# One core's vision tower: 128-row solve of a delta-rule scan, 64-column products in place of narrow ones, and products of ones moved into waits

## The chip, the core and the metric

The kernel runs on one core of a Trainium2 chip. TensorE (PE) multiplies matrices, VectorE (DVE) and ScalarE (ACT) work on rows, GpSimd (POOL) adds, and SyncE (SP) issues the transfers. The metric is the device time of the core in microseconds. Everything is float32. An f32 product on PE is two LDWEIGHTS/MATMUL pairs, so the profile counts two MATMUL records for each call of `mm`.

## The reference, cut to what matters

64 images of 84 x 84 pixels become 4 patch tokens and one class token each, with C = 256 channels: a convolution, attention over nine positions of each window, and a class attention. Then two layers of an attention with a delta rule, each followed by a gated product with 704 inner channels, and at the end a feed-forward part whose operands are rounded to FP4 values. The delta rule runs over sequences of 64 steps and 8 heads of 32 channels:

```python
def step(S, inps):
    qi, ki, vi, bi = inps
    pred = jnp.einsum('bhkv,bhk->bhv', S, ki)
    S = S + bi[..., None, None] * ki[..., :, None] * (vi - pred)[..., None, :]
    o = jnp.einsum('bhkv,bhk->bhv', S, qi)
    return (S, o)
...
for l in range(L):
    h = rmsnorm(x, norm1_w[l])
    x = x + delta_attn(h, Wq[l], Wk[l], Wv[l], Wb[l], Wo[l], onorm_w[l])
    h = rmsnorm(x, norm2_w[l])
    gy = h @ Wg[l]
    g, y = jnp.split(gy, 2, axis=-1)
    x = x + jax.nn.silu(g) * y @ Wd[l]
```

## The kernel before

The order of every engine's work is written out by hand, and semaphores join the engines. PE has one list: the convolution (six groups, L1313), keys and values of the nine positions (L1357, L1371), statistics (`stat`, L1345), class attention (`both_windows`, L1416 and L1420), two times `layer(l)`, and the last stage (L1860 to L1926). PE is mostly fed in time by the others.

The scan over 64 steps is not run step by step. For each of 40 pairs of sequence group and head (NG = 20 column groups on two halves of the partitions) the kernel forms the 64 x 64 matrix of key products, `per_window` (L1707), and solves a triangular system. The 64 steps are two blocks of 32 rows. So the 128 partitions hold four quarters of 32 rows: quarters 0 and 2 are the early blocks, 1 and 3 the late ones. Each half of the 20 groups (b = 0, 1, NB = 10 groups) lies in a PSUM bank of its own.

- The inverse T of each 32 x 32 block is made by doubling in a loop, `pe.Fori(0, LEVELS - 1)`, four rounds: `level_y` (L1736) for both halves, ACT copies (L503), `level_z` (L1745) for both halves, and DVE's masked copy and transpose (L1158, L1161). Each half of each is 40 products of 32 x 32, on all four quarters, 80 records. In the code the loop stands once: 320 record pairs.
- After the loop PE makes the query norms' first halves, two products of 320 columns (L1760, banks 2 and 3).
- `solve((0, 2), b)` (L1767) multiplies T with the values on the early quarters, 20 products for each half. ACT copies quarter 0 (L545), DVE quarter 2 (L1178), 32 rows each.
- The couplings (L1782) give what the early block adds to the late one. DVE adds it in four operations of 32 rows (L1184).
- `solve((1, 3), b)` does the late quarters, with copies by ACT (L548) and DVE (L1188).
- `outputs(0)`, `outputs(1)` (L1801), 40 products. ACT squares them (L551), two products with `blk` complete the norms (L1813), ACT takes Ln and Exp (L329, L331), DVE scales (L1198), PE projects (L1819) and DVE adds the residual (L1203). Between L1198 and L1203 DVE rounds a piece of the FP4 weights (L670, L674, L675). `weights_across` (L1458) are transposes of those weights.

Ahead of the loop stand the projections, `betas` (L1676, L1680; 8 and 4 columns), `key_squares` (L1689, L1691; 4 columns), `per_window`, and the value products (L1720 and L1723, then L1727). `keep_clock` (L1471) and `keep_clock_briefly` (L1476) are products of ones that nobody reads.

## Time and profile before

| what | us |
|---|---|
| median of three runs | 298.47 |
| the three runs | 296.54, 298.47, 299.1 |
| profiled execution, device time | 295.59 |
| its span, first to last instruction | 293.8 |
| mean granted TensorE clock in it | 0.959 of 2.4 GHz |

Times in the rows below are microseconds from the start of the span. A row of the timeline merges neighbouring instructions of one line: start, busy time, engine, line, operation, tiles, rows*columns of the array, shapes, number of records; in brackets the engine's idle time before the first of them and what ended it. "issue" means that the profile shows nothing that the engine waited for.

### The profile page before, as it was taken

To read this page: it belongs to the slowest core of one execution; us is meant where nothing else is said; L and a number is where in the kernel's file an instruction comes from. 1 tells how busy PE (TensorE), PEld (TensorE's weight loads), DVE (VectorE), ACT (ScalarE), POOL (GpSimd) and SP (SyncE) were. 2 spreads that over 40 slices of the span, in tenths; PEclk is the share of its full clock that TensorE was granted. 3 is DMA by queue.
4 is the path that set the end of the run, shared out by engine and by line. 5 is a ranking of instruction groups with operands and counts; after the bars stand their busy time and mean duration, and the time that the engine had idled before them with its cause. 6 is when DMAs were issued, how large, how long until landed. Compare 5 with 4: busy or idle time off the path is not lost.

```text
span 293.8 us, 9910 instructions
## 1 busy us (share of the span) xinstructions
PE 268.0 (91%) x4473; PEld 205.8 (70%) x4473; DVE 201.4 (69%) x402; ACT 96.9 (33%) x243; POOL 38.0 (13%) x35
## 2 busy tenths in 40 slices
PE   8999999999999899968879999978889999788855
PEld 8566678778997788857756766858776676655543
DVE  3649869977689666467668588466676663688761
ACT  1122301330000126656134432755324423462310
POOL 1991100203992000000000000000000000000000
PEclk9999999999999999999959999897995999999988
DMA  7999900000000000000004006200000000000001
GB/s 287 417 424 418 444 20 0 0 0 2 0 0 2 1 2 1 2 4 0 4 2 140 7 1 220 85 2 2 1 7 0 0 2 0 1 0 2 0 10 34
DMA packets 2730, 18.71 MB, mean 64 GB/s; under 512 B 464, under 2 KB 784, under 8 KB 1936
## 3 DMA queue, kind: packets, MB, share of 16 engines
q1 hardware_dynamic: 2704, 18.34, 15.8%
q8 instruction: 20, 0.33, 0.4%
q14 instruction: 6, 0.05, 0.1%
HBM read 18.01 MB, written 0.33 MB: 62 GB/s over the span
## 4 chain that ended last, share of the span: by engine, by line
PE 77%; DVE 14%; ACT 4%; issue 2%; DMA 2%; SPq 0%; DVEq 0%
PE ps L1313 12%; PE ps L1635 8%; PE ps L1357 5%; PE ps L1847 4%; PE ps L1371 4%; PE ps L1889 3%; PE ps L1616 3%; PE ps L1736 3%; PE ps L1745 3%; DMA big<-in_patches 2%; DVE big L1161 2%; DVE wt L1158 2%; PE ps L1303 2%; PE ps L1813 2%; PE ps L1819 2%
## 5 line engine op out<-in xcount | busy, mean ns | idle before, releaser
L1313 PE MATMUL ps<-big,cwb 128*128 128x384 f32 x112 | 37.9, 489 | 0.0
L1313 PEld LDWEIGHTS ps<-big,cwb 128*128 128x128 f32 x112 | 20.9, 190 | 13.0 <-DVE cwb L766 0.3
L1635 PE MATMUL ps<-xT,wl 128*128 128x320 f32 x88 | 24.5, 434 | 1.1 <-ACT wguT L373 1.1
L293 POOL TENSOR_TENSOR xs<-xs,big 128x640 f32<-128x640 f32 x14 | 23.3, 1665 | 1.4
L1635 PEld LDWEIGHTS ps<-xT,wl 128*128 128x128 f32 x88 | 16.6, 190 | 8.2 <-ACT wguT L373 1.6
L1736 PE MATMUL ps<-wt,big 32*32 32x32 f32 x1280 | 14.7, 199 | 5.2 <-DVE wt L1115 2.4
L349 ACT COPY pecT<-ps 128x384 f32<-128x384 f32 x12 | 5.7, 479 | 40.7 <-PE ps L1313 40.7
L1736 PEld LDWEIGHTS ps<-wt,big 32*32 32x32 f32 x1280 | 13.1, 110 | 7.4 <-DVE big L1161 4.0
L1371 PE MATMUL ps<-wt,pecT 128*128 128x256 f32 x72 | 16.5, 381 | 0.6 <-DVE big L871 0.6
L1357 PE MATMUL ps<-wt,pecT 128*128 128x256 f32 x72 | 16.9, 381 | 0.0
L1158 DVE COPY_PREDICATED wt<-cst,ps 128x320 f32<-128x320 int32 x16 | 8.0, 500 | 11.5 <-PE ps L1745 11.5
L1371 PEld LDWEIGHTS ps<-wt,pecT 128*128 128x128 f32 x72 | 13.5, 190 | 2.9 <-DVE big L871 1.0
L1357 PEld LDWEIGHTS ps<-wt,pecT 128*128 128x128 f32 x72 | 13.5, 190 | 2.3
L1745 PE MATMUL ps<-wt,big 32*32 32x32 f32 x1280 | 13.4, 196 | 1.4 <-issue 1.4
L1745 PEld LDWEIGHTS ps<-wt,big 32*32 32x32 f32 x1280 | 12.5, 107 | 1.6 <-issue 1.6
L1847 PE MATMUL ps<-big,wl 128*128 128x320 f32 x48 | 13.4, 435 | 0.0
L776 DVE TENSOR_REDUCE part<-pecT 128x128 f32<-128x384 f32 x12 | 7.1, 594 | 8.7 <-ACT pecT L349 8.6
L1219 DVE TENSOR_TENSOR cwb<-ps,cwb 128x320 f32<-128x320 f32 (+1 forms) x12 | 5.9, 490 | 9.9 <-PE ps L1635 5.7
L1847 PEld LDWEIGHTS ps<-big,wl 128*128 128x128 f32 x48 | 8.8, 190 | 4.2 <-DVE big L1211 1.0
L503 ACT COPY wt<-ps 128x320 f32<-128x320 f32 x16 | 6.8, 425 | 14.6 <-PE ps L1736 14.6
L300 POOL TENSOR_TENSOR sq<-sq 128x384 f32<-128x384 f32 x6 | 6.3, 1051 | 39.9 <-ACT sq L342 39.9
L1889 PE MATMUL ps<-wguT,pecT 128*128 128x352 f32 x32 | 10.0, 466 | 1.1 <-ACT pecT L596 1.1
(310 smaller groups left out, 533.8 us busy)
## 6 DMA issues: line engine op xcount, KB each, us to landing
big<-in_patches SPq DMA_DIRECT2D x6, 960.0 KB, 11.8
wl<-in_layers SPq DMA_DIRECT2D x2, 2176.0 KB, 19.8
wf<-in_ffn SPq DMA_DIRECT2D x1, 2112.0 KB, 17.8
wl<-in_layers SPq DMA_DIRECT2D x2, 1040.0 KB, 15.9
wt<-in_tok SPq DMA_DIRECT2D x1, 1536.0 KB, 24.7
wt<-in_tok SPq DMA_DIRECT2D x1, 768.0 KB, 8.4
cwb<-in_conv SPq DMA_DIRECT2D x1, 640.0 KB, 3.9
cst<-in_constants SPq DMA_DIRECT2D x1, 320.0 KB, 25.0
```

Of the source, the lines that this page charges most:

```text
L293: nc.gpsimd.tensor_tensor(xs[:, hf], old, new, ALU.add).then_inc(S["xsum"], 1)
L776: step(v.tensor_reduce(part[:, min(g % 3, 1), c, :], pecT[:, c, g * GRP:(g + 1) * GRP].rearrange("p (t n) -> p n t", t=3), AX.X, ALU.add))
L1158: v.copy_predicated(tc_[:, g, :], m.unsqueeze(1).broadcast_to([P, NB, 32]), bank32(6 + b, slice(0, P))).then_inc(S["tp"], 1)
L1313: last = mm(ps[:, i % 4, 0:GRP], cwc[:, k, c * P:(c + 1) * P], xg[:, g, k, :], start=(k == 0), stop=(k == KC - 1))
L1357: last = mm(ps[:, 4 + un % 2, t * C:(t + 1) * C], pecT[:, c, i * P:(i + 1) * P], wkv[:, c, 0:C], start=(c == 0), stop=(c == CH - 1))
L1371: last = mm(ps[:, un % 3, t * C:(t + 1) * C], pecT[:, c, i * P:(i + 1) * P], wkv[:, c, C:2 * C], start=(c == 0), stop=(c == CH - 1))
L1616: last = mm(ps[:, bank, cols], lw(at)[:, c, j * P:(j + 1) * P], src[:, c, cols], start=(c == 0), stop=(c == CH - 1))
L1635: last = mm(ps[:, bank, 0:NT], w(c, j), x[:, c, :], start=(c == 0), stop=(c == CH - 1))
L1736: last = mm(ps[r, 4 + b, 32 * k:32 * k + 32], apm[r, NB * b + k, own], tc_[r, NB * b + k, :], start=True, stop=True)
L1745: last = mm(ps[r, 6 + b, 32 * k:32 * k + 32], ttc[r, NB * b + k, :], yc[r, NB * b + k, :], start=True, stop=True)
L1847: last = mm(ps[:, 6 + j, 0:NT], wd[:, i, j * P:(j + 1) * P], act[:, i, :], start=(i == 0), stop=(i == FC - 1))
L1889: last = mm(ps[:, b + w, 0:352], xqT[:, c, P * p:P * p + P], wguT[:, c, 352 * w:352 * w + 352], start=(c == 0), stop=(c == CH - 1))
```

## The change

1. The solve. `solve(b)` works on all four quarters, both times, so the first one also makes unused values on the late quarters and the second one repeats the early ones. One ACT copy of 128 rows takes half b = 0, one DVE copy of 128 rows half b = 1, both times. For the additions to cover 128 rows, the couplings get a second product for each old one, with a stationary operand of zeros (`nought`), which writes zeros under the early quarters; one DVE addition replaces two. The query norms' second product moves behind the second solve.
2. 64 columns (`WIDE`) replace 1, 4 or 8 moving columns where nobody reads the further ones: `stat`, the first products of `both_windows`, `betas` (the first four), `key_squares`, and the norms of the last stage (L1866). `ug` moves into a stretch of `wt` so that 64 columns can be read.
3. Products of ones: 512 instead of 192 columns in the front ahead of `group_scores(1)`; 512 columns between the value products of each layer; 256 columns behind the outputs of each layer; in the last stage two of seven go between the weight transposes, and 256 columns come behind the first output product.
4. ACT makes the causal masks 8 to 11 before its first copy of the loop instead of after.

```diff
+WIDE = 64
+        nought = sb("nought", [P, 32])
-        ug = sb("ug", [P, CH, H])
+        ug = wt[:, T_GQ:T_GQ + 512].rearrange("p (c n) -> p c n", c=CH)
-        def half(x, q, b):
-
-            return x[32 * q:32 * q + 32, NB * b:NB * (b + 1), :].rearrange("p g n -> p (g n)")
+        def part_of(x, b):
+
+            return x[:, NB * b:NB * (b + 1), :].rearrange("p g n -> p (g n)")
-        heads = blk.rearrange("p (h d) -> p h d", h=HP)[:, :, 0]
+        heads = blk.rearrange("p (h d) -> p h d", h=HP)[:, :, 0:WIDE // HP]
...
+            nc.gpsimd.memset(nought[:, :], 0.0)
...
+                causal(8, 12)
                 y_out(1, 0)
...
-                causal(8, 12)
                 y_out(1, 1)
...
-                for b in range(2):
-                    act_.wait_ge(S["u1_mm"], EACH["u1_mm"] * l + b + 1)
-                    nc.scalar.copy(half(uc, 0, b), ps[0:32, 4 + b, 0:NT]).then_inc(S["u1"], 1)
-                for b in range(2):
-                    act_.wait_ge(S["u2_mm"], EACH["u2_mm"] * l + b + 1)
-                    nc.scalar.copy(half(uc, 1, b), ps[32:64, 4 + b, 0:NT]).then_inc(S["u2"], 1)
+                act_.wait_ge(S["u1_mm"], EACH["u1_mm"] * l + 1)
+                nc.scalar.copy(part_of(uc, 0), ps[:, 4, 0:NT]).then_inc(S["half_0"], 1)
+                act_.wait_ge(S["u2_mm"], EACH["u2_mm"] * l + 1)
+                nc.scalar.copy(part_of(uc, 0), ps[:, 4, 0:NT]).then_inc(S["half_0"], 1)
...
-                v.tensor_scalar(nsse, ps[:, 0, 0:NG], EPS_RMS, -1.0, ALU.add, ALU.mult).then_inc(S["ss"], 1)
+                sums = ps[:, 0, 0:PJ * WIDE].rearrange("p (g d) -> p g d", g=NG)[:, :, 0]
+                v.tensor_scalar(nsse, sums, EPS_RMS, -1.0, ALU.add, ALU.mult).then_inc(S["ss"], 1)
...
-                for b in range(2):
-                    dve.wait_ge(S["u1_mm"], EACH["u1_mm"] * l + b + 1)
-                    v.tensor_copy(half(uc, 2, b), ps[64:96, 4 + b, 0:NT]).then_inc(S["u1_two"], 1)
-
+                dve.wait_ge(S["u1_mm"], EACH["u1_mm"] * l + 2)
+                v.tensor_copy(part_of(uc, 1), ps[:, 5, 0:NT]).then_inc(S["half_1"], 1)
                 for b in range(2):
                     dve.wait_ge(S["r_mm"], EACH["r_mm"] * l + b + 1)
-                    for a in range(2):
-                        q = 2 * a + 1
-                        v.tensor_tensor(half(bv, q, b), half(bv, q, b), ps[32 * q:32 * q + 32, 6 + b, 0:NT], ALU.add
-                                        ).then_inc(S["b2"], 1)
-                for b in range(2):
-                    dve.wait_ge(S["u2_mm"], EACH["u2_mm"] * l + b + 1)
-                    v.tensor_copy(half(uc, 3, b), ps[96:128, 4 + b, 0:NT]).then_inc(S["u2_two"], 1)
+                    v.tensor_tensor(part_of(bv, b), part_of(bv, b), ps[:, 6 + b, 0:NT], ALU.add
+                                    ).then_inc(S["half_1"], 1)
+                dve.wait_ge(S["u2_mm"], EACH["u2_mm"] * l + 2)
+                v.tensor_copy(part_of(uc, 1), ps[:, 5, 0:NT]).then_inc(S["half_1"], 1)
...
-                    last = mm(ps[:, 7, at:at + 1], sq[:, 0, t * P:(t + 1) * P], ones[:, 0:1], start=True, stop=True)
+                    last = mm(ps[:, 7, at:at + WIDE], sq[:, 0, t * P:(t + 1) * P], ones[:, 0:WIDE], start=True, stop=True)
...
-                    mm(ps[:, b, at:at + n], stat[:, c, P * hf:P * hf + P], moving(c), start=(c == 0), stop=(c == CH - 1))
+                    mm(ps[:, b, at:at + WIDE], stat[:, c, P * hf:P * hf + P], moving(c, WIDE), start=(c == 0),
+                       stop=(c == CH - 1))
...
-            keep_clock(0, 1, 192)
+            keep_clock(0, 1, 512)
...
-                            last = mm(ps[:, 5, H * p:H * p + H], hT[:, c, P * p:P * p + P], wb[:, c, :],
+                            at = L_B + H * c
+                            last = mm(ps[:, 5, H * p:H * p + WIDE], hT[:, c, P * p:P * p + P], wl[:, at:at + WIDE],
...
-                        mm(ps[:, 0, HP * pj:HP * pj + HP], kqsq[:, 0, pj % 2, P * p:P * p + P], heads, start=True, stop=True)
+                        mm(ps[:, 0, WIDE * pj:WIDE * (pj + 1)], kqsq[:, 0, pj % 2, P * p:P * p + P], heads, start=True,
+                           stop=True)
...
                 last.then_inc(S["v_mm"], 1)
+                keep_clock(5, 1, 512)
                 for c in range(CH):
                     last = mm(ps[:, 7, 0:C], hT[:, c, 0:P], wvb[:, c, :, 0:P], start=(c == 0), stop=(c == CH - 1))
...
-                for j in range(CH):
+
+                def query_norms(j):
+
                     mm(ps[:, 2 + j, 0:NT], blk, kqsq[:, 1, j, :], start=True, stop=False)
 
-                def solve(rows, b):
+                query_norms(0)
+
+                def solve(b):
 
                     for g in range(NB * b, NB * (b + 1)):
-                        for q in rows:
+                        for q in range(4):
...
-                    solve((0, 2), b).then_inc(S["u1_mm"], 1)
+                    solve(b).then_inc(S["u1_mm"], 1)
                 pe.sem_inc(S["t"], -2)
                 for b in range(2):
-                    pe.wait_ge(S["u1"], EACH["u1"] * l + b + 1)
-                    pe.wait_ge(S["u1_two"], EACH["u1_two"] * l + b + 1)
+                    if b:
+                        pe.wait_ge(S["half_1"], EACH["half_1"] * l + 1)
+                    else:
+                        pe.wait_ge(S["half_0"], EACH["half_0"] * l + 1)
                     for g in range(NB * b, NB * (b + 1)):
+                        cols = slice(32 * (g % NB), 32 * (g % NB) + 32)
                         for a in range(2):
-                            last = mm(ps[64 * a + 32:64 * a + 64, 6 + b, 32 * (g % NB):32 * (g % NB) + 32],
-                                      apm[64 * a:64 * a + 32, g, 32:64], uc[64 * a:64 * a + 32, g, :],
-                                      start=True, stop=True)
+                            early, late = slice(64 * a, 64 * a + 32), slice(64 * a + 32, 64 * a + 64)
+                            mm(ps[early, 6 + b, cols], nought[late, :], uc[late, g, :], start=True, stop=True)
+                            last = mm(ps[late, 6 + b, cols], apm[early, g, 32:64], uc[early, g, :], start=True, stop=True)
                     last.then_inc(S["r_mm"], 1)
                 for b in range(2):
-                    pe.wait_ge(S["b2"], EACH["b2"] * l + 2 * b + 2)
-                    solve((1, 3), b).then_inc(S["u2_mm"], 1)
+                    pe.wait_ge(S["half_1"], EACH["half_1"] * l + b + 2)
+                    solve(b).then_inc(S["u2_mm"], 1)
+                query_norms(1)
+
...
                 outputs(1).then_inc(S["o_mm"], 2)
+                keep_clock(5, 1, 256)
...
-            weights_across(6, 9)
-            keep_clock(5, 7)
+            weights_across(6, 8)
+            keep_clock(5, 2)
+            weights_across(8, 9)
+            keep_clock(5, 5)
...
                 last.then_inc(S["out_mm"], 1)
+                if p == 0:
+                    keep_clock(4, 1, 256)
```

## Rows read from the trace of the kernel before

**Rows 1.** The page: busy time of the engines (part 1), DMA queues (3), the chain (4).
```profile
PE 268.0 (91%) x4473; PEld 205.8 (70%) x4473; DVE 201.4 (69%) x402; ACT 96.9 (33%) x243; POOL 38.0 (13%) x35
...
q8 instruction: 20, 0.33, 0.4%
...
PE 77%; DVE 14%; ACT 4%; issue 2%; DMA 2%; SPq 0%; DVEq 0%
```

**Rows 2.** PE's timeline from the loop's end; the last line is layer 1.
```profile
140.07 1.57 PE L1745 MATMUL ps<-wt,big 32*32 32x32 f32 x160
141.88 1.31 PE L1760 MATMUL ps<-pecT,cst 128*128 128x320 f32 x4 [0.24 <-issue]
143.13 1.45 PE L1767 MATMUL ps<-wt,big 32*32 32x32 f32 x80
...
149.32 1.70 PE L1801 MATMUL ps<-big,wt 64*32 64x64 f32 x80 [0.69 <-DVE wt L1188]
151.61 2.50 PE L1813 MATMUL ps<-wt,cst 128*128 128x320 f32 x4 [0.59 <-ACT wt L551]
...
219.09 1.60 PE L1801 MATMUL ps<-big,wt 64*32 64x64 f32 x80 [0.69 <-DVE wt L1188]
```

**Rows 3.** DVE's timeline in the same stretch of layer 0.
```profile
145.49 2.04 DVE L1184 TENSOR_TENSOR wt<-wt,ps 32x320 f32<-32x320 f32 x4 [0.37 <-PE ps L1782]
...
155.12 0.55 DVE L1198 SCALAR_TENSOR_TENSOR big<-ps,vec,wt 128x320 f32<-128x320 f32 x1 [0.45 <-ACT wt L331]
```

**Rows 4.** PE's timeline where it stops on "issue"; the last four are layer 1.
```profile
127.67 0.89 PE L1736 MATMUL ps<-wt,big 32*32 32x32 f32 x80 [1.40 <-DVE wt L1115]
...
129.26 1.20 PE L1745 MATMUL ps<-wt,big 32*32 32x32 f32 x115 [0.28 <-issue]
...
197.09 0.50 PE L1745 MATMUL ps<-wt,big 32*32 32x32 f32 x36
198.70 1.65 PE L1745 MATMUL ps<-wt,big 32*32 32x32 f32 x124 [1.11 <-issue]
...
214.62 0.88 PE L1782 MATMUL ps<-wt,big 32*32 32x32 f32 x44
215.66 0.76 PE L1782 MATMUL ps<-wt,big 32*32 32x32 f32 x36 [0.15 <-issue]
```

**Rows 5.** Windows: stretch, length, busy time of engines, granted clock, DMA share, GB/s.
```profile
126.90:127.10 0.20, 0.00 (x0) 0.00 (x0) 0.17 (x1) 0.20 (x2) 0.00 (x0) 1.00 0.31 82
130.30:130.50 0.20, 0.17 (x18) 0.05 (x6) 0.17 (x2) 0.03 (x1) 0.00 (x0) 1.00 0.35 82
131.00:142.00 11.00, 9.64 (x961) 9.00 (x962) 7.83 (x17) 5.91 (x19) 0.00 (x0) 1.00 0.00 0
143.10:143.30 0.20, 0.20 (x11) 0.17 (x12) 0.00 (x0) 0.00 (x0) 0.00 (x0) 1.00 0.27 82
...
195.80:196.00 0.20, 0.00 (x0) 0.00 (x0) 0.20 (x1) 0.20 (x2) 0.00 (x0) 1.00 0.45 82
...
213.10:213.30 0.20, 0.20 (x12) 0.18 (x13) 0.00 (x0) 0.00 (x0) 0.00 (x0) 1.00 0.32 82
```

**Rows 6.** The page's granted clock in 40 slices (7.3 us each), and two windows.
```profile
PEclk9999999999999999999959999897995999999988
...
148.00:154.70 6.70, 5.36 (x114) 3.88 (x109) 4.27 (x7) 2.61 (x7) 0.00 (x0) 0.50 0.01 2
...
189.00:192.30 3.30, 3.30 (x83) 2.64 (x72) 1.51 (x4) 2.50 (x9) 0.00 (x0) 0.50 0.02 5
```

**Rows 7.** PE's timeline: one-column and 64-column products, and L1707 in both layers.
```profile
45.31 2.07 PE L1345 MATMUL ps<-ones,sq 128*128 128x1 f32 x18
...
111.32 1.10 PE L1605 MATMUL ps<-gag,wt 128*128 128x64 f32 x8
...
121.05 1.56 PE L1707 MATMUL ps<-pecT 32*64 32x128 f32 x80
...
188.78 2.44 PE L1707 MATMUL ps<-pecT 32*64 32x128 f32 x80
```

More of the change, by code:

```diff
@@ L930, in class_keys @@
                 dve.wait_ge(S["u"], 1)
-                v.tensor_tensor(ug[:, :, :], u[:, :, :],
+                v.tensor_tensor(ug[:, :, 0:H], u[:, :, :],
                                 vec[:, V_GKG:V_GKG + 2].unsqueeze(2).broadcast_to([P, CH, H]), ALU.mult
@@ L1419, in both_windows @@
                     for c in range(CH):
-                        last = mm(ps[64 * a:64 * a + 64, b, at + n:at + 2 * n], stat[:, c, cols], moving(c),
+                        last = mm(ps[64 * a:64 * a + 64, b, at + n:at + 2 * n], stat[:, c, cols], moving(c, n),
                                   start=(c == 0), stop=(c == CH - 1))
@@ L1428, in group_scores @@
                 pe.wait_ge(S["k_free"], 10)
-                both_windows(5, 2 * H * hf, H, lc[:, 1], lambda c: ug[:, c, :], hf).then_inc(S["gsc_mm"], 1)
+                both_windows(5, 2 * H * hf, H, lc[:, 1], lambda c, n: ug[:, c, 0:n], hf).then_inc(S["gsc_mm"], 1)
             def group_stats(hf):
@@ L1436, in group_stats @@
                     pe.wait_ge(S["rk"], 4)
-                both_windows(7, 100 + 2 * hf, 1, sql, lambda c: ones[:, 0:1], hf).then_inc(S["gst_mm"], 1)
+                both_windows(7, 100 + 2 * hf, 1, sql, lambda c, n: ones[:, 0:n], hf).then_inc(S["gst_mm"], 1)
             def group_values(hf):
@@ L1688, in key_squares @@
                         p = pj // 2
-                        mm(ps[:, 0, HP * pj:HP * pj + HP], kqsq[:, 0, pj % 2, P * p:P * p + P], heads, start=True, stop=True)
+                        mm(ps[:, 0, WIDE * pj:WIDE * (pj + 1)], kqsq[:, 0, pj % 2, P * p:P * p + P], heads, start=True,
+                           stop=True)
                     for a in range(2):
-                        last = mm(ps[64 * a:64 * a + 64, 0, 4 * HP:5 * HP], kqsq[:, 0, a, NW:NT], heads, start=True, stop=True)
+                        last = mm(ps[64 * a:64 * a + 64, 0, 4 * WIDE:5 * WIDE], kqsq[:, 0, a, NW:NT], heads, start=True,
+                                  stop=True)
                     last.then_inc(S["ss_mm"], 1)
@@ L1803, in outputs @@
                     return last
-                for b in range(2):
-                    pe.wait_ge(S["u2"], EACH["u2"] * l + b + 1)
-                pe.wait_ge(S["u2_two"], EACH["u2_two"] * l + 2)
+                pe.wait_ge(S["half_0"], EACH["half_0"] * (l + 1))
+                pe.wait_ge(S["half_1"], EACH["half_1"] * (l + 1))
                 outputs(0).then_inc(S["o_first"], 1)
@@ L1865, in _ @@
                     n = P if p < 2 else 64
-                    last = mm(ps[0:n, p, 0:1], sqx[:, c, P * p:P * p + n], ones[:, 0:1], start=(c == 0), stop=(c == CH - 1))
+                    last = mm(ps[0:n, p, 0:WIDE], sqx[:, c, P * p:P * p + n], ones[:, 0:WIDE], start=(c == 0),
+                              stop=(c == CH - 1))
                     if c and p:
```

2 lines of the change are left out of this document (1 added, 1 removed).

## The prediction

> **What bounds the kernel now.** I read the page's totals first, then the chain of waits, then PE's timeline between the end of the doubling loop and the next projection. PE is busy for 91% of the span [rows 1] and the chain that ended last is PE's for 77% of it [rows 1], so the time is that of PE's list. The solve is a thinner place. In layer 0 the loop ends at 140.07 + 1.57 = 141.64, two wide products follow, then the 32x32 products of the first solve (80 records in L1767), the couplings L1782 (80), the second solve (80), and the outputs L1801, which start at 149.32 [rows 2]: 7.7 us for 244 records, most of it waiting for 32-row copies and additions such as the four of L1184, 2.04 us together [rows 3]. (An f32 product is two records.) The second thing to see is the granted clock: 0.50 (the 1.2 GHz level) from 148.0 to 154.7 and from 189.0 to 192.3, and by the slices of the page also near 199 to 203, near 220 to 226 and near the end [rows 6]. So it falls after both solves and after the tiny products of layer 1. The third thing is where the forecast is decided: PE's instructions arrive as a stream. The page counts 20 pieces of kind "instruction" with 0.33 MB, 16.4 KB each [rows 1]. Of 4,473 records 3 x 320 x 2 are repeats of a loop, so 2,553 stand in the code, 128 to a piece.
>
> Three times PE stopped in dense code with nothing to wait for ("issue"): inside L1745 in layer 0 for 0.28 us, at its record 36 in layer 1 for 1.11 us, and at record 44 of L1782 in layer 1 for 0.15 us [rows 4]. From the second stop to the third lie, in code, some 43 + 80 records of L1745, 4 of L1760, 80 of L1767 and 44 of L1782: 251, two pieces of 126 (a piece holds waits too). Each stop ends a fixed time after a piece began to land: pieces begin near 127.0, 195.9 and 213.2 [rows 5], PE goes on at 129.26, 198.70 and 215.66 [rows 4], so 2.3, 2.8 and 2.5 us later. After the first stop the next piece begins near 130.4 [rows 5], 1.1 us after PE went on. So I read: on entering piece k PE asks for piece k+1 alone, it begins to land 1.1 us later and can be used 3.35, 3.9 and 3.55 us after the request. No piece arrives while the loop repeats (0 GB/s from 131 to 142) [rows 5].
>
> **The change part by part.**
> (a) Solves on all four quarters. Records per layer: first solve 80 to 160, couplings 80 to 160 (the products of zeros), second solve 80 to 160, outputs 80. With four quarters 160 records took 1.57 us [rows 2], 9.8 ns each; with two, 80 took 1.45 us, 18 ns. So in array time twice the products cost nothing: 6 blocks of 0.78 us, 4.7 us. One 128-row copy replaces two 32-row ones, and one addition two, since 32 rows take as long (2.04 / 4 = 0.51 us in L1184) as 128 (0.55 in L1198) [rows 3]. One product of query norms, some 0.6 us [rows 2], moves behind the second solve, beside DVE's last copy. If code is free, outputs start 0.9 + 4.7 = 5.6 us plus 0.4 after 141.64, at 147.65 instead of 149.32: 1.7 us won per layer.
>
> But the same stretch is then 2 + 160 + 160 + 160 + 2 + 80 records straight through, 564 instead of 324. In layer 0 a piece began near 143.2 [rows 5], so PE entered piece A near 142.1, some ten records behind the loop; the next borders come 126, 252, 378 and 504 records later, the last at about record 30 of the outputs. A piece's content needs 126 x 9.8 ns = 1.2 us and the next one 3.4 us, so PE stops in every piece. B opens at 142.1 + 3.4 = 145.5 (in the first solve), C at 148.9 (couplings), D at 152.3 (second solve), E at 155.5 to 155.7. The last 50 records of the outputs, at the 21 to 24 ns that they show at the lower clock (80 in 1.70) [rows 2], end near 156.6. Before, they ended at 151.02; the following L1813 had its start at 151.61 and comes to 157.4: +5.8 us. Layer 1: A at 213.2 - 1.1 = 212.1, E at 212.1 + 4 x 3.5 = 226.1, outputs end at 227.2 instead of 219.09 + 1.60 = 220.69 [rows 2]: +6.5, and 0.2 for (c). Together +12.5 us. This puts code in the place of the copies' waits, which all fit into the stops. Behind the outputs nothing is denser than before. ACT's Ln and Exp, DVE's L1198, its three steps of weight rounding and the two additions of L1203 keep their distances.
>
> (b) Clock around the solves. In full-speed code (a) would also hold the clock at 2.4 GHz, worth about 1.2 us per layer: L1813 takes 2.50 us for what takes 1.31 in L1760 at the upper level [rows 2], and DVE's weight rounding between L1198 and L1203 takes part of that back. With stops in each piece PE has 1.2 us of work in 3.4 us, and the clock fell before in a stretch that held more, so I count nothing won.
>
> (c) Wide products of ones. 256 columns behind the outputs last 0.43 us at full clock, covered by the wait for ACT's square (0.59 us ahead of L1813) [rows 2]; at half clock 0.85, so 0.2 to 0.3 sticks out, counted above. 512 columns between the value products: 0.85 us under PE's wait for DVE, 1.40 us in layer 0 [rows 4]. But L1736's first half starts 0.8 us later, and in it PE enters the piece whose successor it then lacks in L1745; the request and the end of that stop move by about 0.75 us in layer 0. The front's 512 instead of 192: +0.05. In the last stage seven stay seven, and the new 256 lies in a wait for DVE: 0. Its fall at the end stays.
>
> (d) Columns 1, 4 or 8 made 64. Eighteen one-column records take 2.07 us, eight 64-column ones 1.10 us; less the 0.2 us that the end of the last one adds, 104 and 113 ns each [rows 7]. 104 records are widened (36 of L1345, 16 of the two windows, 16 betas, 24 squares of keys, 12 at the end): 1.0 us at most, nothing if the weight load sets the pace; I take 0.6, on the side of the row. In return the fall at 189.0 [rows 6], behind these products, should go: 80 records of L1707 would take 1.56 instead of 2.44 us [rows 7], -0.9, of which (c) gives back 0.4 as the code request is later; and the fall near 199 goes with the filled wait, -0.5 (an estimate: L1745 and L1736 are held back there less by the clock than by DVE).
>
> (e) Moving ug into wt, the order of ACT's causal masks, strided reads: covered by PE, 0.
>
> Sum on the profiled execution: 295.59 + 12.5 + 0.75 + 0.05 + 0.6 - 0.5 - 0.5 = 308.5 us. The runs' median, 298.47, is 2.9 above that execution. I carry 1 us of this over, since clock falls placed by chance will also be in the new one, and say 309.5. With 3.3 to 3.9 us per piece over eight pieces the sum moves by -1 to +3.5; with (d) at its ends by 0.6; so 305 to 315 for this case alone.
>
> A rule that speaks against my reading: the Trainium skill, "Runtime: NRT & Kernel Launch", section "Instruction fetch mechanics", says that code comes in 16 KiB blocks of 256 instructions, the next one fetched while the current one runs, and that this is mostly hidden because issue is slower than the refill. The size agrees (16.4 KB, 128 pairs). "Hidden" does not, at 9.8 ns a record: the three stops say so. By that rule the time would be that of the first rival.
>
> **The rivals.**
> 1. Code is on time (the stops of rows 4 have another cause, or several pieces can be asked for). For it: 160 records ran at 9.8 ns, and the chain gives "issue" 2% [rows 1]. Against it: those 160 were mostly a repeated loop, and the stops stand 251 records apart. Then: 2 x 1.7 won in the solves, 2 x 1.2 by the clock (DVE's rounding included), 1.4 by the falls at 189 and 199, 0.7 paid: 295.6 - 6.5 = 289, and with the offset 290 to 291. It is decided by whether a stretch of over 126 records in straight code at under 27 ns runs through. Faster.
> 2. Code delays only part: requests go out earlier since the queue runs ahead during waits, a piece takes 2 to 2.7 us instead of 3.4. Then E opens 8 to 10.8 us after 142.1 and the outputs end at 151 to 154, 0 to 2.7 us later than before in each layer: 297 to 302.
> 3. Widened columns cost 30 ns instead of 6, with the first rival's solve: 292 to 294.
> 4. The change doesn't do what it says (128-row operations cost more than 32-row ones): excluded by [rows 3].
>
> **How the numbers follow.** Forecast 0.72; rival 2 0.08 (half of it slower by over 1%, half within); rivals 1 and 3 together 0.20, of which 0.01 ends within 1%. Measurement can tell about 1% from no change. Slower 0.76, same 0.06, faster 0.18. The range reaches from 298 to 316: it holds the forecast's 305 to 315 and most of rival 2, and leaves out the first rival and tails, 0.2.
>
> **What would show it.** Right: in the solve PE has five pieces landing about 3.5 us apart, idle time of about 2 us called "issue" in the first solve, the couplings, the second solve and the outputs, and from the loop's end to L1813's counterpart 16 us instead of 10. Wrong: solve blocks back to back in under 6 us, pieces landing 1.5 us apart, and clock 1.0 behind the solves. The fall at 189 gone shows (d); the first stop of L1745 about 0.7 us longer in layer 0 shows (c).

## The result, and the profile after

| | before | after |
|---|---|---|
| median of the paired runs, us | 298.79 (4 runs) | 311.7 (4 runs) |
| lowest and highest, us | 296.54, 300.32 | 309.67, 312.33 |
| profiled execution, its span | 295.59, 293.8 | 309.67, 307.9 |
| mean granted TensorE clock in it | 0.959 | 0.945 |

The ratio is 1.0385, with a 95% interval from 1.0277 to 1.0493: the medians differ by 12.9 us, the profiled executions by 14.1 us. A fifth run of the changed kernel, outside the paired ones, took 307.38 us. Some runs of either kernel fall into a slower state, and the ratios, here and below, are those of the others.

The page of the changed kernel, the lines that answer to [rows 1] (busy time, the queue of code, the chain), and two of its groups of instructions: L1747 is the doubling loop's second part, L1773 the solve. After the bar stand busy time, mean ns of one, and the idle time before them with what ended it.

```profile
PE 275.1 (89%) x4963; PEld 209.0 (68%) x4963; DVE 197.5 (64%) x394; ACT 95.3 (31%) x239; POOL 38.0 (12%) x36
...
q8 instruction: 24, 0.39, 0.5%
...
PE 75%; DVE 14%; issue 6%; ACT 4%; POOL 0%; DVEq 0%; POOLq 0%
...
L1747 PE MATMUL ps<-wt,big 32*32 32x32 f32 x1280 | 13.5, 197 | 2.7 <-issue 2.7
L1773 PE MATMUL ps<-wt,big 32*32 32x32 f32 x640 | 8.9, 215 | 6.4 <-issue 6.4
```

PE has 490 more records and is busy 7.1 us longer, but the span grew by 14.1. "issue" on the chain went from 2% to 6%, and the solve alone lost 6.4 us to it. PE's timeline from the loop's end in layer 0, the answer to [rows 2]; the couplings L1792/L1793 alternate, and one of their rows stands for all, the one where PE went on after its stop:

```profile
143.03 0.78 PE L1764 MATMUL ps<-pecT,cst 128*128 128x320 f32 x2 [0.24 <-issue]
143.73 1.36 PE L1773 MATMUL ps<-wt,big 32*32 32x32 f32 x134
146.70 0.41 PE L1773 MATMUL ps<-wt,big 32*32 32x32 f32 x26 [1.60 <-issue]
...
150.30 0.26 PE L1793 MATMUL ps<-wt,big 32*32 32x32 f32 x1 [2.20 <-issue]
...
153.76 1.48 PE L1773 MATMUL ps<-wt,big 32*32 32x32 f32 x90 [1.57 <-issue]
155.17 1.44 PE L1764 MATMUL ps<-pecT,cst 128*128 128x320 f32 x2
156.53 1.95 PE L1812 MATMUL ps<-big,wt 64*32 64x64 f32 x80
158.41 1.22 PE L1469 MATMUL ps<-cst,ones 128*128 128x256 f32 x2
159.43 2.34 PE L1824 MATMUL ps<-wt,cst 128*128 128x320 f32 x4
```

Three stops of 1.60, 2.20 and 1.57 us, with nothing that PE waited for. Layer 1 has the same three (at 223.02, 226.89 and 230.35, of 1.60, 2.09 and 1.58 us). Windows of the same trace, each where a piece of PE's code begins to land in layer 0 (stretch, length, busy time of PE, its weight loads, DVE, ACT, POOL, granted clock, DMA share, GB/s):

```profile
144.20:144.40 0.20, 0.20 (x45) 0.20 (x36) 0.00 (x0) 0.00 (x0) 0.00 (x0) 1.00 0.29 82
147.90:148.10 0.20, 0.20 (x22) 0.08 (x10) 0.20 (x1) 0.00 (x0) 0.00 (x0) 1.00 0.30 82
151.30:151.50 0.20, 0.20 (x33) 0.20 (x25) 0.10 (x1) 0.00 (x0) 0.00 (x0) 0.50 0.35 82
154.80:155.00 0.20, 0.20 (x29) 0.20 (x19) 0.00 (x0) 0.00 (x0) 0.00 (x0) 0.50 0.33 82
158.20:158.40 0.20, 0.20 (x24) 0.04 (x6) 0.17 (x2) 0.00 (x0) 0.00 (x0) 0.50 0.29 82
```

Narrower windows put their beginnings at 144.33, 147.97, 151.43, 154.89 and 158.28, 3.4 to 3.6 us apart. PE goes on at 146.70, 150.30 and 153.76, which is 2.3 to 2.4 us after a piece began to land; before, 2.3 to 2.8 us were read from [rows 4, 5]. From one stop to the next PE runs 128 records (136 from the loop's end to the first stop, then 128 and 128). In the kernel before, the pieces behind the loop of layer 0 began at 143.2, 146.85 and 150.6, also about 3.7 us apart, but there PE ran out of them only once, for 0.15 us in layer 1 [rows 4].

Where the 14.1 us lie, by the start of the same work in the two traces (for the loop, the end of its last product), each time after less before:

| milestone | before | after | gap | grown by |
|---|---|---|---|---|
| first half of the loop's first product, layer 0 | 125.4 | 126.4 | 1.0 | 1.0 |
| loop's end, layer 0 | 141.6 | 142.8 | 1.2 | 0.2 |
| norms (L1813; L1824) | 151.6 | 159.4 | 7.8 | 6.6 |
| `per_window`, layer 1 | 188.8 | 196.6 | 7.8 | 0.0 |
| first half of the loop's first product, layer 1 | 194.4 | 201.7 | 7.3 | -0.5 |
| loop's end, layer 1 | 211.6 | 219.1 | 7.5 | 0.2 |
| norms, layer 1 | 221.3 | 235.3 | 14.0 | 6.5 |
| down projection, layer 1 | 241.9 | 254.5 | 12.6 | -1.4 |
| last output product's end | 291.0 | 305.1 | 14.1 | 1.5 |

So 13.1 of 14.1 us arise between the loops' ends and the norms.

### The profile page after: what moved, and what is told of

It is laid out like the page before. It is cut to its first block, busy times and chain, and to the rows that moved or that the text cites. A ratio compares the mean times of both kernels' runs of the same rounds, so it can differ in the third digit from the quotient of the medians.

```text
span 307.9 us, 10875 instructions
## 1 busy us (share of the span) xinstructions
PE 275.1 (89%) x4963; PEld 209.0 (68%) x4963; DVE 197.5 (64%) x394; ACT 95.3 (31%) x239; POOL 38.0 (12%) x36
## 4 chain that ended last, share of the span: by engine, by line
PE 75%; DVE 14%; issue 6%; ACT 4%; POOL 0%; DVEq 0%; POOLq 0%
PE ps L1310 12%; PE ps L1633 8%; PE ps L1354 5%; PE ps L1858 4%; PE ps L1368 3%; PE ps L1903 3%; PE ps L1614 3%; PE ps L1738 3%; PE ps L1773 3%; PE ps L1747 3%; PE ps L1474 2%; DVE big L1163 2%; PE ps L1937 2%; PE ps L1469 2%; DVE wt L1160 2%
## 5 line engine op out<-in xcount | busy, mean ns | idle before, releaser
L1633 PEld LDWEIGHTS ps<-xT,wl 128*128 128x128 f32 x88 | 16.6, 190 | 9.1 <-ACT wguT L376 2.4
L1738 PE MATMUL ps<-wt,big 32*32 32x32 f32 x1280 | 14.6, 198 | 4.1 <-DVE big L1163 2.4
L1738 PEld LDWEIGHTS ps<-wt,big 32*32 32x32 f32 x1280 | 12.9, 109 | 6.3 <-DVE big L1163 4.0
L1160 DVE COPY_PREDICATED wt<-cst,ps 128x320 f32<-128x320 int32 x16 | 8.0, 500 | 12.9 <-PE ps L1747 12.8
L1747 PE MATMUL ps<-wt,big 32*32 32x32 f32 x1280 | 13.5, 197 | 2.7 <-issue 2.7
L1773 PE MATMUL ps<-wt,big 32*32 32x32 f32 x640 | 8.9, 215 | 6.4 <-issue 6.4
L1747 PEld LDWEIGHTS ps<-wt,big 32*32 32x32 f32 x1280 | 12.6, 108 | 2.9 <-issue 2.9
L1469 PE MATMUL ps<-cst,ones 128*128 128x320 f32 (+2 forms) x36 | 13.7, 491 | 0.0
L1858 PE MATMUL ps<-big,wl 128*128 128x320 f32 x48 | 13.4, 435 | 0.0
L1773 PEld LDWEIGHTS ps<-wt,big 32*32 32x32 f32 x640 | 7.9, 125 | 7.7 <-issue 7.7
L506 ACT COPY wt<-ps 128x320 f32<-128x320 f32 x16 | 6.8, 426 | 16.4 <-PE ps L1738 16.4
## 6 DMA issues: line engine op xcount, KB each, us to landing
wf<-in_ffn SPq DMA_DIRECT2D x1, 2112.0 KB, 17.9
```

The lines of the kernel that those rows point to most:

```text
L1160: v.copy_predicated(tc_[:, g, :], m.unsqueeze(1).broadcast_to([P, NB, 32]), bank32(6 + b, slice(0, P))).then_inc(S["tp"], 1)
L1469: mm(ps[:, bank, 0:width], ones[:, :], cst[:, 0:width], start=True, stop=True)
L1633: last = mm(ps[:, bank, 0:NT], w(c, j), x[:, c, :], start=(c == 0), stop=(c == CH - 1))
L1738: last = mm(ps[r, 4 + b, 32 * k:32 * k + 32], apm[r, NB * b + k, own], tc_[r, NB * b + k, :], start=True, stop=True)
L1747: last = mm(ps[r, 6 + b, 32 * k:32 * k + 32], ttc[r, NB * b + k, :], yc[r, NB * b + k, :], start=True, stop=True)
L1773: last = mm(ps[r, 4 + b, 32 * (g % NB):32 * (g % NB) + 32], ttc[r, g, :], bv[r, g, :], start=True, stop=True)
```

## The experiments

The theory: PE's code comes in pieces of 16.4 KB (128 records with their weight loads, a few less where waits and a loop's end stand between them), one ahead at most, 3.4 to 3.9 us apart when PE would use them up faster, and the change grows the straight code behind each loop from 324 to 564 records. Rivals: the doubled products or the longer copies cost by themselves; the granted clock makes the loss; the wide products of ones do.

**1. The solve alone** (edit 1, without the wide products and the 64 columns).

```diff
-                    solve((0, 2), b).then_inc(S["u1_mm"], 1)
+                    solve(b).then_inc(S["u1_mm"], 1)
...
+                            mm(ps[early, 6 + b, cols], nought[late, :], uc[late, g, :], start=True, stop=True)
...
-                    solve((1, 3), b).then_inc(S["u2_mm"], 1)
+                    solve(b).then_inc(S["u2_mm"], 1)
```

> Only the solve is changed (four quarters, products of zeros, 128-row copies and additions, query norms split); columns, products of ones and the mask order are those of before. If code arrival is the cause (564 instead of 324 records behind each loop, some 27 ns a record), the kernel is as slow as the whole change: about 12 to 13 us over before, 310 to 312, with four stops on issue behind each loop. If the rest of the change (64 columns, products of ones) is the cause, it is at before's time less 3 us, 295 to 299.

Measured: 308.21 us (4 runs) against 297.84 (13 runs), ratio 1.0328 with an interval from 1.0257 to 1.0399. The solve carries most of the loss, but 2 us less of it than expected. The profiled execution took 312.53 us, more than the other three, so I take only places from it: stops in the first solve, the couplings and the second solve, and in layer 0 a short one (0.46 us) in the outputs.

**2. Everything but the solve** (edits 2 to 4; before's solve put back).

```diff
-                    solve(b).then_inc(S["u1_mm"], 1)
+                    solve((0, 2), b).then_inc(S["u1_mm"], 1)
...
+                    nc.scalar.copy(half(uc, 0, b), ps[0:32, 4 + b, 0:NT]).then_inc(S["u1"], 1)
```

> Everything but the solve is changed. Code arrival: within 1% of before, 298 to 300: the first stop in L1745 0.8 us longer in each layer, the low clock behind the narrow products of layer 1 gone, 0.6 us for wider columns. If the rest is the cause of the loss: 308 to 312.

Measured: 302.76 us (4 runs), ratio 1.0141 (1.0074 to 1.0209): 4 to 5 us, where the forecast's sum had 0.4. The expectation, 298 to 300 us, was missed. From the loops' ends to the norms it takes 10.6 and 10.8 us, before 10.0 and 9.7; the new product of 256 columns stands in this stretch, at the lower clock 1.22 us long in a wait of 0.59 us. PE's timeline of this kernel at the first stop in layer 0 and at layer 1's loop (L1743 and L1752 are the loop's two products):

```profile
129.45 0.56 PE L1752 MATMUL ps<-wt,big 32*32 32x32 f32 x43
131.37 1.22 PE L1752 MATMUL ps<-wt,big 32*32 32x32 f32 x117 [1.36 <-issue]
133.06 2.35 PE L1743 MATMUL ps<-wt,big 32*32 32x32 f32 x160 [0.47 <-DVE big L1163]
...
199.58 0.45 PE L1752 MATMUL ps<-wt,big 32*32 32x32 f32 x30
200.98 1.79 PE L1752 MATMUL ps<-wt,big 32*32 32x32 f32 x128 [0.95 <-issue]
204.43 0.26 PE L1752 MATMUL ps<-wt,big 32*32 32x32 f32 x2 [1.67 <-issue]
```

In layer 0 the stop is 1.36 us instead of 0.28 [rows 4]. In layer 1 a second border falls into the loop's first pass, two records before its end, and costs 1.67 us that neither before nor after paid. Three products of ones, six records, stand more in the code ahead of this place; before, the stop came after record 36 (now 30), and the rest of the pass, 124 records, ran through [rows 4].

**3. Between the two: the whole change with 404 records behind each loop** (the first solve stays on four quarters, no products of zeros, the second solve on two quarters).

```diff
-                            mm(ps[early, 6 + b, cols], nought[late, :], uc[late, g, :], start=True, stop=True)
...
-                    solve(b).then_inc(S["u2_mm"], 1)
+                    solve(b, (1, 3)).then_inc(S["u2_mm"], 1)
```

> The changed kernel without the products of zeros and with the second solve on the late quarters alone (the values added to the early quarters are then read by nobody): 404 records behind each loop instead of 564, all 128-row copies and additions kept. Code arrival: 160 x 27 ns = 4.3 us less in each layer, 302 to 304. If the products' own time on the array counts (9.8 ns a record, or the waits of copies): 160 x 9.8 ns = 1.6 us less in each layer, 308 to 309.

Measured: 305.68 us (4 runs), ratio 1.0269 (1.0208 to 1.033). The time lies between the two expectations. From loop's end to norms: 13.4 us in both layers. With the whole change (16.6 and 16.2) and experiment 2 (10.6 and 10.8), 564, 404 and 324 records take 16.4, 13.4 and 10.7 us in the mean: 240 records cost 5.7 us, 24 ns each, but unevenly, the first 80 of them 34 ns each and the other 160 19 ns, where 27 ns were expected for each. A piece of 128 records each 3.5 us would be 27 ns. Products that are left out take no array time either, so this alone doesn't separate code from products; experiments 5 and 6 do.

**4. The whole change with 324 records behind each loop** (both solves on two quarters, the 128-row copies and additions kept).

```diff
-                    solve(b).then_inc(S["u1_mm"], 1)
+                    solve(b, (0, 2)).then_inc(S["u1_mm"], 1)
...
-                            mm(ps[early, 6 + b, cols], nought[late, :], uc[late, g, :], start=True, stop=True)
...
-                    solve(b).then_inc(S["u2_mm"], 1)
+                    solve(b, (1, 3)).then_inc(S["u2_mm"], 1)
```

The further rows that the copies take here carry values that nobody reads.

> As the one before, and the first solve on the early quarters alone: 324 records as before the change, with 128-row copies and additions (they also carry values that nobody reads). Code arrival: some 7 us less in each layer than the changed kernel, and against the kernel with the rest alone only 0.5 to 1 us a layer, since the code of 324 records (8.7 us) sets the pace: 297 to 298.5. If copies set the pace: 1.7 us less in each layer than the rest alone, 295 to 296.

Measured: 298.46 us (11 runs), ratio 1.0013 (0.9972 to 1.0055). Taking the 240 records away gives back the whole 13 us, with every copy at 128 rows. Long copies are not the loss. This kernel differs from that of experiment 2 (1.0141) only in the solve's copies, additions and the place of one query-norm product; experiment 9 finds 0.2% for the copies and additions alone. So the prices of the parts don't simply add, and why this one is 1.3% faster was not taken apart.

**5 and 6. The same 256 tiny products, straight and in a loop**, put into the kernel before ahead of the layers, where nothing waits for them. Their values are read by nobody.

```diff
+            tiny_products(256)
```

```diff
+            with pe.Fori(0, 4):
+                tiny_products(64)
```

> The kernel before with 256 more 32x32 products of ones (512 records, unread) ahead of layer 0, written out. Price of code by itself. If a piece of 126 records is asked for only when the one ahead of it is entered, their last ones run at 3.4 to 3.9 us per 126 records: the stretch takes 12 to 14 us, broken by three or four stops on issue of about 2 us, with pieces landing about 3.4 us apart. If code is on time: 512 x 9.8 ns = 5.0 us without a stop.

> The same 512 records as a loop of four rounds over 64 products (128 records in the code). If code arrival sets the pace: one stop at most in the first round, then rounds of 1.25 us plus the branches, 6 to 9 us in all, so 5 to 7 us less than written out. If the products' own time sets the pace: both take the same.

Measured, one execution each: 314.1 and 304.88 us. PE's timeline of the straight ones:

```profile
115.33 2.09 PE L1855 MATMUL ps<-ones 32*32 32x32 f32 x225
119.73 1.27 PE L1855 MATMUL ps<-ones 32*32 32x32 f32 x128 [2.31 <-issue]
123.45 1.93 PE L1855 MATMUL ps<-ones 32*32 32x32 f32 x128 [2.46 <-issue]
127.18 0.65 PE L1855 MATMUL ps<-ones 32*32 32x32 f32 x31 [1.80 <-issue]
```

and of the looped ones:

```profile
117.22 1.29 PE L1855 MATMUL ps<-ones 32*32 32x32 f32 x128
118.66 4.10 PE L1855 MATMUL ps<-ones 32*32 32x32 f32 x384 [0.16 <-issue]
```

The 512 records take 12.5 us in straight code and 5.5 us in the loop. The straight ones come in bursts of exactly 128 behind a first one of 225 (the rest of one piece and the whole next one), with 3.7 us from the start of one to the next (119.73, 123.45, 127.18). Engine, waits, operands and products are the same in the two. One thing follows from the stops: the granted clock is 1.00 throughout the loop and 0.50 from 122 on in the straight code, where a burst takes 1.93 instead of 1.27 us. That is 0.7 us in this burst, and the three stops are 6.6 us together. What costs is that the code is new. The whole kernels differ by 9.2 us; the 2.2 us outside this stretch were not followed up.

**7. The borders moved.** 45 products of ones instead of 35 at the start of the kernel, in a wait: 20 records more ahead of everything, so every border comes 20 records earlier.

```diff
-            keep_clock_briefly(7, 35)
+            for _ in range(45):
+                mm(ps[0:32, 7, 0:50], ones[:, 0:32], ones[:, 0:50], start=True, stop=True)
```

> The changed kernel with ten more small products (20 records) at the very start, where PE waits for the first patches (45 of 50 columns in place of 35 of 64): everything behind lies 20 records later against the borders of the code pieces. Code arrival: the first stop in the loop's second product group moves from record 43 to 47 to about record 23 to 27, a new stop of about 2 us appears near record 310 of the loop's first round, and behind the loop the stop at record 134 of the first solve is gone, the others come 20 records earlier; 1.6 us are lost in each loop and 1.7 won behind it, so the time stays within 1% of the changed kernel, 309 to 312. If the stops have to do with what is computed there, they stay at the same products.

Measured: 311.07 us (4 runs), ratio 1.0488 (1.0437 to 1.0538). PE's timeline (L1748 is the loop's second product, L1774 the first solve):

```profile
128.77 0.38 PE L1748 MATMUL ps<-wt,big 32*32 32x32 f32 x23
130.10 1.30 PE L1748 MATMUL ps<-wt,big 32*32 32x32 f32 x128 [0.95 <-issue]
134.10 0.28 PE L1748 MATMUL ps<-wt,big 32*32 32x32 f32 x9 [2.70 <-issue]
...
147.20 1.58 PE L1774 MATMUL ps<-wt,big 32*32 32x32 f32 x160
```

The stop after record 43 of the loop's product moved to record 23, 20 earlier. A new stop of 2.70 us appeared 128 records on, inside the loop's first pass, and the stop in the first solve is gone in layer 0: its 160 records run through. In layer 1 it moved from record 139 to 119. The stops follow the borders, not the work. The expected balance did not come out: the loops' first passes lost more, and the ratio is 1.0% above that of the whole change.

**8. The clock held up in the stops.** After the first half of the first solve and behind each half of the couplings a product of ones, 512 columns wide.

```diff
+                    if b == 0:
+                        keep_clock(0, 1, 512)
...
+                    keep_clock(0, 1, 512)
```

> The changed kernel with one product of ones of 512 columns behind the first half of the first solve and behind each half of the couplings, placed into the stops: tells the clock from the code. If code sets the pace, the pieces stay 3.4 to 3.6 us apart and only what runs at the lower clock behind the solve (second query norm, outputs, norms, transposes) gets shorter: 1 to 2 us less in each layer, 308 to 310. If the low clock is what makes the solve slow: 6 us less in each layer, 300.

Measured: 308.9 us (4 runs), ratio 1.0396 (1.033 to 1.0461). The page's clock slices of this kernel:

```profile
PEclk9999999999999999999989999999997999999979
```

The mean clock rose to 0.982, above the 0.959 of the kernel before, and the ratio is that of the whole change. From the loops' ends to the norms it took 17.1 and 16.4 us, although the clock was low for 3.4 us there in layer 0 and hardly at all in layer 1 (with the change as it is, about 11 and 10 us). In layer 1 the pieces still began 3.3 to 3.8 us apart. In layer 0 they were 3.3 to 4.2 us apart, since the three products take time of their own. The low clock accompanies the loss and doesn't make it. What the clock gives is read behind the norms of layer 0: from there to the down projection it took 19.1 us, with the change as it is 19.9.

**9. The 128-row copies and additions alone**, in the kernel before, with its 324 records behind each loop and no further products.

```diff
-                for b in range(2):
-                    dve.wait_ge(S["u1_mm"], EACH["u1_mm"] * l + b + 1)
-                    v.tensor_copy(half(uc, 2, b), ps[64:96, 4 + b, 0:NT]).then_inc(S["u1_two"], 1)
+                dve.wait_ge(S["u1_mm"], EACH["u1_mm"] * l + 2)
+                v.tensor_copy(part_of(uc, 1), ps[:, 5, 0:NT]).then_inc(S["half_1"], 1)
...
-                        v.tensor_tensor(half(bv, q, b), half(bv, q, b), ps[32 * q:32 * q + 32, 6 + b, 0:NT], ALU.add
+                    v.tensor_tensor(part_of(bv, b), part_of(bv, b), ps[:, 6 + b, 0:NT], ALU.add
```

The late quarters' rows in the first copies, and the early ones' in the additions, carry values that nobody reads.

> The kernel before with one change: 128-row copies and additions in the solve, the products and their count as before (324 records behind each loop); the further rows carry values that nobody reads. If copies set the pace of the solve, 1.7 us less in each layer: 294 to 295. If code arrival takes over once the copies are short (324 records need about 8.7 us, the stretch takes 10.0 now): 0.5 to 1 us less in each layer, 296 to 297.

Measured: 296.53 us (12 runs) against 297.33 (17 runs), ratio 0.9983 (0.9948 to 1.0018). PE's timeline (L1765 solve, L1784 couplings, L1802 outputs):

```profile
144.10 1.45 PE L1765 MATMUL ps<-wt,big 32*32 32x32 f32 x80
145.44 1.14 PE L1784 MATMUL ps<-wt,big 32*32 32x32 f32 x54
147.09 0.59 PE L1784 MATMUL ps<-wt,big 32*32 32x32 f32 x21 [0.51 <-issue]
...
147.63 2.16 PE L1765 MATMUL ps<-wt,big 32*32 32x32 f32 x74
150.48 1.70 PE L1802 MATMUL ps<-big,wt 64*32 64x64 f32 x80 [0.69 <-DVE wt L1181]
```

(Some records are missing from this trace.) PE waits for no copy or addition until the outputs, but it stops for 0.51 us on its code, and the second solve's 74 records take 2.16 us at the lower clock, which came at 147.4. The outputs start 7.9 us behind the loop's end (142.61), against 7.7 before [rows 2]; in layer 1 it is 7.2 against 7.5.

**10. Experiment 2 without the 512 columns between the value products.**

```diff
-                keep_clock(5, 1, 512)
```

> The kernel with everything but the solve changed (measured at 1.014 of before), without the 512 columns of ones between the value products. If these cost by the later code request (first stop in L1745 longer by 0.8 to 1.3 us) and by the lower clock that follows it in the loop: 3 us less, 299 to 300, and no clock fall inside the loop of layer 0. If the 64-column products are what costs: no change, 302 to 303.

Measured: 296.5 us (10 runs) against 296.69 (23 runs), ratio 0.9977 (0.9945 to 1.001). That is 3 us below what was expected. The one product of 512 columns in each layer carries the whole 1.4% of experiment 2. PE's timeline of this kernel in the two layers:

```profile
129.01 0.58 PE L1751 MATMUL ps<-wt,big 32*32 32x32 f32 x45
130.19 1.58 PE L1751 MATMUL ps<-wt,big 32*32 32x32 f32 x115 [0.61 <-issue]
...
197.38 0.47 PE L1751 MATMUL ps<-wt,big 32*32 32x32 f32 x34
198.54 1.77 PE L1751 MATMUL ps<-wt,big 32*32 32x32 f32 x126 [0.70 <-issue]
```

The stops are 0.61 and 0.70 us, against 1.36 and 0.95 + 1.67 in experiment 2. In layer 1 the border that experiment 2 met two records before the end of the pass now lies just behind it. The second half of the expectation was wrong: the clock does fall inside the loop of layer 0, from 130.6 to 134.0, for as long as in experiment 2 (133.0 to 136.4). In layer 1 it is low for 3.4 us instead of 6.8. The stops explain 2.7 of the 6.0 us between the two traces, and another 1.7 us lie in the last stage, where the clock was low from 266.2 to 269.5 in experiment 2 and not here; what made that fall isn't shown. The 64-column products are all still in: with the fall at 189 that went with them, they cost nothing that can be measured.

**11. The clock kept without delaying the loop**: the kernel before with edit 2's 64 columns (all but `stat`), edit 4, and three products of ones of 256 columns in waits of the solve (behind the couplings, behind the second solve, behind the outputs).

```diff
+                keep_clock(0, 1, 256)
                 for b in range(2):
                     pe.wait_ge(S["b2"], EACH["b2"] * l + 2 * b + 2)
                     solve((1, 3), b).then_inc(S["u2_mm"], 1)
+                keep_clock(0, 1, 256)
...
+                keep_clock(5, 1, 256)
```

> The kernel before with products of ones of 256 columns in three waits of the solve (behind the couplings, the second solve and the outputs; 6 records a layer), and 64 columns in betas, key squares and the class windows, nothing else. If the clock can be kept up behind the solve at so little code: the falls at 148 and 220 are gone or shorter, L1813 takes 1.1 to 1.3 us instead of 2.5, the fall at 189 is gone, 2 to 4 us less: 294 to 296. If code arrival takes it back (stop in the couplings longer): 297 to 298.

Measured: 296.24 us (12 runs) against 296.69 (23 runs), ratio 0.9983 (0.9953 to 1.0013), just above the first expectation. The norms ran at the upper level:

```profile
153.14 0.70 PE L1474 MATMUL ps<-cst,ones 128*128 128x256 f32 x2
153.83 1.34 PE L1823 MATMUL ps<-wt,cst 128*128 128x320 f32 x4
```

1.34 us for what took 2.50 [rows 2], and from the loop's end to the down projection 28.6 us in both layers against 30.0 and 30.2 before. But the clock was low from 129.6 to 136.4 and from 197.9 to 208 instead, inside the loops. In this trace the gain went there: from the loop's first product to its end it took 17.9 and 19.5 us in the two layers, before 16.2 and 17.2.

**12. Experiments 9 and 11 together**: the short chain of copies with the clock kept, one product of ones behind the second solve and one behind the outputs.

```diff
-                keep_clock(0, 1, 256)
                 for b in range(2):
-                    pe.wait_ge(S["b2"], EACH["b2"] * l + 2 * b + 2)
-                    solve((1, 3), b).then_inc(S["u2_mm"], 1)
+                    pe.wait_ge(S["half_1"], EACH["half_1"] * l + b + 2)
+                    solve(b, (1, 3)).then_inc(S["u2_mm"], 1)
                 keep_clock(0, 1, 256)
```

> The two harmless halves together: before's sparse solve (324 records behind each loop) with 128-row copies and additions as in the run of the copies alone (1.00 of before), and the clock held through the solve by products of ones 256 columns wide in its waits as in the run with the clock kept (1.00 of before). Each alone gave nothing back at the end of the kernel. If what the copies save (two copies and two additions per layer fewer in a row, 0.5 to 1 us per layer) had only been lost to the low clock that followed, it shows now: 294.5 to 295.5 us against 296.7, ratio 0.993 to 0.996. If the code stop in the second part of the solve and the falls of the clock inside the loop take it back as they did in the two runs: 296 to 297.5, ratio 0.997 to 1.003.

Measured: 294.31 us (6 runs) against 297.31 (11 runs), ratio 0.9899 (0.9839 to 0.9958). It beats the kernel before by 1.0%, a little more than expected, and stands 4.9% of before's time below the changed one. PE's timeline of layer 1:

```profile
213.02 1.45 PE L1771 MATMUL ps<-wt,big 32*32 32x32 f32 x80
214.36 1.52 PE L1790 MATMUL ps<-wt,big 32*32 32x32 f32 x80
215.77 1.52 PE L1771 MATMUL ps<-wt,big 32*32 32x32 f32 x80
217.23 0.70 PE L1467 MATMUL ps<-cst,ones 128*128 128x256 f32 x2
217.98 1.44 PE L1809 MATMUL ps<-big,wt 64*32 64x64 f32 x80
219.35 0.70 PE L1467 MATMUL ps<-cst,ones 128*128 128x256 f32 x2
220.03 1.34 PE L1821 MATMUL ps<-wt,cst 128*128 128x320 f32 x4
```

This is what edit 1 was after, with half of the changed solve's products: solve, couplings and second solve back to back, norms 8.6 us behind the loop's end (9.7 before) and at the upper level. In layer 0 the clock still fell at 129.3 and at 149.8, and the norms came 9.7 us behind the loop. That the fall in layer 1's loop stayed away here and not in experiment 11 wasn't taken apart.

## Why the prediction was right, and where its terms were off

**Sign and mechanism: right.** The forecast was pieces about 3.5 us apart, PE stopped in the solve, the couplings and the second solve, and 16 us instead of 10 from the loop's end to the norms. Measured were 16.6 and 16.2 us, with pieces at 144.33, 147.97, 151.43, 154.89 and 158.28, 3.4 to 3.6 us apart. Of the four stops forecast behind each loop three came; the one in the outputs stayed away (see (a)). The runs leave no rival beside it: the same products cost 5.5 us looped and 12.5 straight (experiments 5 and 6), the stops move with the borders (7), without the 240 records the loss is gone (4), and with the clock at 0.982 it stays (8).

**The size of a piece** was taken at 126 records. That came from a stretch that holds a loop's end and waits; behind the loop it was 128, and the borders still fell within a few records of their forecast places.

**Rival 1 (code is on time) fell** by the stops at the borders. Its test, "a stretch of over 126 records runs through", was set too low, since the rest of one piece and the whole next one can be there already: 134 records ran through in the first solve, 160 in that of experiment 7 and 225 in experiment 5, and behind each PE stopped. The Trainium skill, "Runtime: NRT & Kernel Launch", section "Instruction fetch mechanics", calls the crossing of a 16 KiB boundary mostly hidden. In this kernel it is hidden in the first 118 us, the convolution and what follows, where PE shows no wait on "issue"; it costs 1.6 to 2.2 us in the changed solve, where 128 records take 1.3 us.

**Rival 2 (a piece in 2 to 2.7 us) fell**: no two pieces were closer than 3.3 us. **Rival 3 (64 columns cost 30 ns each) fell**: experiment 10 holds all of them and is at 0.9977, and in the last stage six records of one column took 0.81 us and six of 64 columns 0.92 (L1866, now L1877), 18 ns more each. **Rival 4**: a 128-row copy on DVE took 0.49 us (L1179, L1185) and on ACT 0.43 (L549), as the 32-row ones.

**Terms of the sum.**

- (a) Forecast +5.8 and +6.5 us, measured +6.6 and +6.5. In layer 0 two things were sized wrongly. The moved query-norm product was to lie beside DVE's last copy at 0.6 us; it took 1.44 us at the lower clock and ended behind that copy (155.28 + 0.49 = 155.77, the product 156.61). And the outputs, forecast to stop once more for piece E, show no stop in the changed kernel: their border fell near 157.2 (the next piece begins to land at 158.28, 1.1 us later), 2.3 us after E began to land at 154.89, when E had just become usable.
- (b) Nothing won by the clock around the solves: right in layer 0 (low from 148.3 to 162.0). In layer 1 it came back at 233.6, before the norms, and gave 1.4 us, which the last stage lost again (low for 6.8 us near the end, before for 3.4).
- (c) The first stop was forecast 0.75 us longer in layer 0: it went from 0.28 to 1.12 us, +0.84. In layer 1 it went from 1.11 to 1.56, +0.45 (forecast 0.4). But in experiments 2 and 10, with before's solve, the same 512 columns made the difference between 1.0141 and 0.9977. The sum had no term for a border that falls into the loop's first pass, or for the clock that falls with a longer stop. Within the whole change part of this is covered: experiments 1 and 2 add to 4.7%, the whole change is 3.85%.
- (d) Taken at 0.6 us; up to `per_window` of layer 0 the trace has 0.3 us (121.35 against 121.05), the front's wider product included. That the fall at 189 [rows 6] goes was right: `per_window` in layer 1 took 1.63 us instead of 2.44 [rows 7]. That the fall near 199 goes, forecast at -0.5 us, was wrong: it came later instead, behind the longer first stop, and just as long. The window in the changed kernel, with the granted clock at 0.50:

```profile
206.30:209.70 3.40, 3.28 (x241) 3.14 (x241) 2.77 (x5) 0.36 (x2) 0.00 (x0) 0.50 0.02 5
```

- The offset from profile to median was carried at 1 us and measured at 2.0 (309.67 against 311.7): the changed kernel's profiled execution was the fastest of the paired runs, and before's was faster than all of its paired ones.
- The chances add up a little differently: half of rival 2 and 0.01 make 0.05 for "same", not 0.06.

The forecast of 309.5 us missed the median by 2.2 us, 1.2 by the sum (308.5 against 309.67) and 1.0 by the offset. That the medians differ by 12.9 us, exactly the sum's growth, is chance: the sum was made for the profiled executions, which differ by 14.1.

## What to carry to other kernels

Count the instruction records between two places where TensorE waits anyway, not only their array time: once the one or two pieces that are already there are used up, straight code of tiny products ran here at 27 to 29 ns a record (128 in 3.5 to 3.7 us), however short each product was, so products that are "free" in array time are not. A loop that repeats the same products paid nothing of this behind its first pass, and a few records more or less ahead of a loop decided whether one more border, with its 1.5 to 2.7 us, fell into the first pass. A filler in a wait is free only if nothing behind it is limited by a request that it delays: here 512 columns, which were to be fully covered by a wait, made 1.4% in experiment 2.

## What the runs showed of the hardware that I had not expected

- The bursts between two stops were exactly 128 records, in code of products alone (experiments 5 and 7) and in the changed solve too.
- The doubling loop, 320 records or 2.5 pieces long, repeats without any code traffic. The step back to its start doesn't show: PE waits there for DVE, 0.47 us in the changed kernel; in the short loop of experiment 6 it shows as 0.16 us of "issue". The Trainium skill, "Runtime: NRT & Kernel Launch", section "Instruction fetch mechanics", says that a taken branch out of a window of two pages forces a fetch; here the branch went back over 2.5 pieces, and in the loop's later rounds no piece came (0 GB/s from 131 to 142) [rows 5].
- 20 records moved at the start of the kernel changed the time from 1.0385 (1.0277 to 1.0493) to 1.0488 (1.0437 to 1.0538) of before. The intervals overlap, but the trace shows one more stop in each loop's first pass, of 2.70 and 1.53 us. An edit far away can act through the place of the borders alone.
- A low clock that is driven out of one place came back in another (experiment 11), and a mean clock of 0.982 bought nothing between the loops' ends and the norms while the code was late (experiment 8).
